# A graph network's preparation on one core: noise embedding and row splits on VectorE, weight pieces behind the tables, edges loaded first, waits on stored counts divided

## What is computed

```python
# cut to what matters; shapes: x [1250, 512], src, dst, edge_weight [21250], node_vec1 [1250, 1]
freqs = jnp.arange(1, 33) * (2.0 * np.pi / 16)
ph = noise_levels * freqs
emb = jnp.concatenate([jnp.sin(ph), jnp.cos(ph)], axis=-1)         # [1250, 64]
cond = silu(emb @ f_w1 + f_b1) @ f_w2 + f_b2                       # [1250, 16]
for i in range(4):
    y = layernorm(x) * (1 + cond @ s1_w[i] + s1_b[i]) + cond @ b1_w[i] + b1_b[i]
    y = sparse_attention(y, src, dst, ...)                         # softmax over each node's edges, 4 heads
    x = x + y
    y = layernorm(x) * (1 + cond @ s2_w[i] + s2_b[i]) + cond @ b2_w[i] + b2_b[i]
    x = x + relu(y @ m_w1[i] + m_b1[i]) @ m_w2[i] + m_b2[i]
x = layernorm(x0 + x)
agg = segment_sum(x[dst] * edge_weight[:, None], src)
return layernorm(x + agg @ weight.T)
```

## Time and profile before

| | |
|---|---|
| median of 3 runs | 1954.78 us (1954.19 to 1955.04) |
| profiled execution | 1956.64 us, its span 1954.8 us |
| granted TensorE clock, mean | 0.97 |
| busy: TensorE, VectorE, ScalarE, GpSimd | 1783.7, 1306.0, 916.6, 423.4 us |
| last group added, tables done | 247.7 us from the start of the span |
| first scores of layer 0 | 313.4 us |

### The profile page before, as it was taken

The page is one execution under the profiler, slowest core; times in us unless marked ns, Lnnn a source line. Parts: engine busy times, 40 slices in busy tenths (PEclk is TensorE's granted clock), DMA queues, the critical chain, the costliest instruction groups (busy, mean ns, idle before and its releaser), DMA issues.

```text
span 1954.8 us, 31300 instructions
## 1 busy us (share of the span) xinstructions
PE 1783.7 (91%) x11879; PEld 1527.7 (78%) x11879; DVE 1306.0 (67%) x2411; ACT 916.6 (47%) x1471; POOL 423.4 (22%) x499
## 2 busy tenths in 40 slices
PE   3447579999999999999999999999999999999898
PEld 3446557888888788888887888888878888888777
DVE  8997785676685655766856567668565676585744
ACT  6557664454454244544542445445424454453221
POOL 5562223000025230000251300002513000024300
PEclk9678789999999999999999999999999999999999
DMA  3020155242231022422410224223102233232122
GB/s 117 11 49 10 57 223 186 85 148 90 85 127 50 16 83 81 142 90 85 133 44 16 88 84 135 96 83 129 44 16 90 76 131 104 88 115 86 40 69 76
DMA packets 63635, 170.06 MB, mean 87 GB/s; under 512 B 5857, under 2 KB 24066, under 8 KB 63485
## 3 DMA queue, kind: packets, MB, share of 16 engines
q10 hardware_dynamic: 23040, 102.41, 15.6%
q1 hardware_dynamic: 40452, 65.69, 10.3%
HBM read 146.58 MB, written 17.02 MB: 84 GB/s over the span
## 4 chain that ended last, share of the span: by engine, by line
PE 75%; DVE 10%; issue 7%; ACT 3%; DMA 2%; DVEq 2%; SPq 1%; POOL 1%; POOLq 0%; ACTq 0%
PE ps L1442 65%; PE ps L1654 8%; DVE onehot L1032 1%; PE ps L1574 1%; DVE prob L1198 1%; DVE PT_lo L1214 1%; DVEq L1056 1%; DVE CW L1068 1%; ACT PT_hi L842 1%; DVE CW L1071 1%; DVE CW L1064 1%; DMA piece<-in_L_gnn_m_w_dram 1%; PE ps L1869 1%; DVE CW L1066 0%; SPq L388 0%
## 5 line engine op out<-in xcount | busy, mean ns | idle before, releaser
L842 ACT ACTIVATE PT_hi<-ps 128x512 fp32r<-128x512 f32 x400 | 238.5, 596 | 245.0 <-PE ps L1654 244.1
L1214 DVE TENSOR_TENSOR PT_lo<-ps,PT_hi 128x512 fp32r<-128x512 f32 x400 | 274.1, 686 | 50.0 <-ACT PT_hi L842 42.4
L826 ACT ACTIVATE prob<-prob,nmax 128x1250 f32<-128x1250 f32 x160 | 214.0, 1338 | 139.0 <-DVE nmax L1198 139.0
L1654 PE MATMUL ps<-ident,prob 128*128 128x128 f32 x1600 | 248.4, 278 | 11.9 <-DVE PT_lo L1214 11.9
L1198 DVE CUSTOM_DVE_ANT_0 prob<-ps,Lr 128x1250 f32<-128x1250 f32 x160 | 232.2, 1451 | 33.6 <-PE ps L1442 32.2
L1654 PEld LDWEIGHTS ps<-ident,prob 128*128 128x128 f32 x1600 | 181.7, 140 | 78.8 <-DVE PT_lo L1214 61.1
L1442 PE MATMUL ps<-PT_hi,v_hi 128*128 128x256 f32 x800 | 228.0, 285 | 1.1 <-DVE PT_lo L1214 1.1
L1442 PE MATMUL ps<-PT_lo,v_hi 128*128 128x256 f32 x800 | 226.1, 283 | 0.0
L1442 PE MATMUL ps<-PT_hi,v_lo 128*128 128x256 f32 x800 | 225.9, 282 | 0.0
L1442 PE MATMUL ps<-yT,wqk_hi 128*128 128x512 f32 (+1 forms) x768 | 213.0, 364 | 4.3 <-DVE yT L1151 4.3
L1442 PE MATMUL ps<-win,onehot 128*128 128x112 bf16 x1680 | 113.8, 240 | 101.0 <-DVE CW L1071 78.3
(11 more groups left out here) (205 smaller groups left out, 3797.5 us busy)
## 6 DMA issues: line engine op xcount, KB each, us to landing
Lr<-l_table ACTq DMA_DIRECT2D x160, 625.0 KB, 3.9
piece<-in_L_gnn_m_w_dram SPq DMA_DIRECT2D x32, 256.0 KB, 2.7
w_table<-CW SPq DMA_DIRECT2D x5, 1250.0 KB, 7.5
l_table<-CW SPq DMA_DIRECT2D x10, 625.0 KB, 3.2
prob<-w_table SPq DMA_DIRECT2D x10, 625.0 KB, 3.9
x<-in_x_dram SPq DMA_DIRECT2D x2, 2304.0 KB
CW<-CW SPq DMA_DIRECT2D x7, 625.0 KB, 5.8
piece<-in_L_gnn_wv_dram SPq DMA_DIRECT2D x16, 256.0 KB, 2.7
```

The lines of the kernel that those rows point to most:

```text
L826: act.activation(buf, buf, ACT.Exp, bias=nmax[:, i % 4:i % 4 + 1], scale=-1.0, accum_out=rsum[:, i % 4:i % 4 + 1]).then_inc(S["exped"], 1)
L842: act.activation(o, i, ACT.Copy).then_inc(S["pt_hi"], 1)
L1214: dve.tensor_tensor(lo, i, hi.bitcast(F32), ALU.subtract).then_inc(S["pt_split"], 1)
L1654: m = pe.transpose(bank(5 + n % 2, at * P, (at + 1) * P), prob[:, (NT * h + 2 * g + j) % 3, d * P:(d + 1) * P], ident[:])
```

## The change

1. **Angles on VectorE.** The embedding's angles are made by VectorE ahead of group 8 (`angles`), with fewer steps, since one instruction multiplies and adds. The nodes are folded into two halves: 128 x 640 in place of 64 x 1280. The sine, the noise matmuls (four in place of three) and the silus move from groups 28 to 32 to groups 12 to 17, the condition from 34 to 18.
2. **Row differences on VectorE**, ahead of groups 16 and 24; ScalarE's casts at groups 6, 22 and 28 in place of 3, 9 and 17.
3. **Weight pieces.** The six pieces are loaded into buffers of their own, without waiting for one another. ScalarE rounds them at groups 44 to 54; GpSimd subtracts all six after `tables_done`.
4. **Edges first.** SyncE loads the edges before it adds START to the semaphores. ScalarE casts `iota_h`; the constant rows of the stacks are copied by SyncE's queue; GpSimd zeroes three tiles, ScalarE nine.
5. **TensorE** turns the biases ahead of group 3 in place of ahead of group 0.
6. **VectorE's loop** is written out in seven parts; five row statistics instead of three are taken ahead of the last eight groups, and the two between the first normed rows are gone.
7. **Divided waits.** Four semaphores count the stores of logarithms in place of two, and `qk_hi_` waits for those that its own columns need. ScalarE's third logarithm and its store come earlier.

```diff
-ZERO_BY_DMA, ZERO_BY_POOL, ZERO_SOURCE = range(7), (7, 8), NT - 1
+ZERO_BY_POOL = ((1, 7), (1, 8), (0, 9))
+ZERO_BY_ACT = range(9)
-L_FIRST = 5
-ACT_L_AT = {1: (2,), 2: (3,), 3: (4,), ...}
+L_STORE = (0, 0, 1, 1, 2, 3, 3, 3, 3, 3)
+L_STORES = (2, 2, 1, 5)
+QK_STORES = {0: (0,), 1: (1,), 4: (2,)}
+ACT_L_AT = {2: (3,), 3: (4,), ...}
-EARLY_STATS = 3
+EARLY_STATS = 5
@@ SyncE
-            for s in counted:
-                sp.sem_inc(s, START)
             sp.wait_ge(pre_set, 2)
...
+            for s in counted_groups:
+                sp.sem_inc(s, START)
             sp.wait_ge(zero_source, 1)
...
+            for s in S.values():
+                sp.sem_inc(s, START)
...
-            for n in range(4):
-                load_piece(0, n)
+            for n in range(AHEAD_PIECES):
+                sp.dma_start(first_raw(n), piece_rows(0, n)).then_inc(first_in[n], 16)
...
-                if n == L_FIRST - 1:
-                    store_weights(4)
+                if n in (1, 2):
+                    store_weights(n + 2)
@@ GpSimd
-            between = {1: (constants, phase), 2: (lambda: row_rest(0), turns), ...}
+            between = {6: (cond_rest,), 9: (last_x,)}
...
+                    if l == 0 and t == EARLY_STATS - 1:
+                        pool.wait_ge(tables_done, 1)
+                        for n in range(AHEAD_PIECES):
+                            first_rest(n)
@@ ScalarE
-            between = {2: (biases,), 3: (lambda: row_hi(0),), 9: (lambda: row_hi(1),), 17: (lambda: row_hi(2),),
-                       24: (lambda: first_hi(0), lambda: first_hi(1)), 28: (sines,), 29: (lambda: silu(0), lambda: silu(1)),
-                       32: (lambda: silu(2),), 35: (cond_copy,), 41: ..., 43: (cond_stack,), 47: ...}
+            between = {4: (biases,), 6: (lambda: row_hi(0),), 12: (sines,), 14: (lambda: silu(0), lambda: silu(1)), 17: (lambda: silu(2), lambda: silu(3)),
+                       20: (cond_copy,), 22: (lambda: row_hi(1),), 28: (lambda: row_hi(2),), 31: (cond_stack,),
+                       **{44 + 2 * n: (lambda n=n: first_hi(n),) for n in range(AHEAD_PIECES)}}
...
                     if l == 0 and h == 0:
-                        act.wait_ge(l_stored1, 16 * L_FIRST)
+                        for i in QK_STORES.get(c, ()):
+                            act.wait_ge(l_stored[i], 16 * L_STORES[i])
...
+                    elif l == 0:
+                        log_counts(2)
@@ VectorE
-            dve.wait_ge(iota_set, 3)
-            link(dve.tensor_copy(iota_h[:], iota_i[:]))
...
+            def angles():
+                dve.wait_ge(noise_in, 32)
+                dve.wait_ge(f_set, 2)
+                dve.wait_ge(iota_set, 8)
+                link(dve.tensor_scalar(fcol[:, 0:1], fcol_i[:], TWO_PI / 16.0, None, ALU.mult))
+                link(dve.tensor_scalar(sin_a[:], sin_a[:], fcol[:, 0:1], None, ALU.mult))
...
+                for c in TURN:
+                    link(dve.scalar_tensor_tensor(out=sin_a[:], in0=sin_b[:], scalar=-c, in1=sin_a[:], op0=ALU.mult, op1=ALU.add))
+                link(dve.tensor_scalar(sin_a[:], sin_a[:], fcol[:, 2:3], PI_IN, ALU.add, ALU.min))
+                dve.tensor_scalar(sin_a[:], sin_a[:], -PI_IN, None, ALU.max).then_inc(sin_ready, 1)
...
+            between = {1: (angles,), 2: (lambda: row_rest(0),), 3: (lambda: row_rest(1),), NG // UNROLL_G - 1: (early_stats,)}
+
+            for i in range(NG // UNROLL_G - 1):
+                for work in between.get(i, ()):
+                    work()
+                with dve.If(flag < 1):
+                    groups(i)
...
-                        if t + 3 < NT:
+                        if EARLY_STATS <= t + 3 < NT:
                             stats(t + 3)
...
-                    first_stats(EARLY_STATS + step - 1)
                     log_table(step - 1)
+            log_table(2)
@@ TensorE
-            between = {29: (lambda: hidden_cond(0), lambda: hidden_cond(1)), 31: (lambda: hidden_cond(2),), 34: (make_cond,), 42: (turn_cond,)}
+            between = {3: (turn_biases,), 12: (lambda: hidden_cond(0), lambda: hidden_cond(1)), 15: (lambda: hidden_cond(2), lambda: hidden_cond(3)), 18: (make_cond,),
+                       29: (turn_cond,)}
```

More of the change, by code:

```diff
@@ L241, in build @@
             wv_hi = sb("wv_hi", [P, KT, D], F32R, start_of_layer)
+            with ExitStack() as prep:
+                wv_raw = sb("wv_raw", [P, KT, D], F32, prep)
             wv_lo = sb("wv_lo", [P, KT, D], F32R, start_of_layer)
@@ L276, in build @@
         piece_in = [sem(f"piece_in{i}") for i in range(2)]
+        first_in = [sem(f"first_in{i}") for i in range(AHEAD_PIECES)]
         stacks1_in, stacks2_in, bo_in = sem("stacks1_in"), sem("stacks2_in"), sem("bo_in")
@@ L297, in build @@
         x0_in = sem("x0_in")
-        l_stored1, l_stored2 = sem("l_stored1"), sem("l_stored2")
+        l_stored = [sem(f"l_stored{i}") for i in range(len(L_STORES))]
         l_in = [sem(f"l_in{i}") for i in range(LBUFS)]
@@ L353, in pieces, with first_raw @@
             return []
+        def first_raw(n):
+            return wv_raw[:, n, :] if n < QKO else wqk_raw[:, n - QKO]
         def piece_parts(n):
@@ L449, in _ @@
             sp.dma_start(x[0:LAST, NT - 1, :], T["x"][(NT - 1) * P:N, :]).then_inc(x_in, 16)
-            for n in range(4, AHEAD_PIECES):
-                load_piece(0, n)
             def store_weights(i):
@@ L598, in last_x @@
                 pool.memset(x[:, NT - 1, :], 0.0).then_inc(f_set, 1)
-            between = {1: (constants, phase), 2: (lambda: row_rest(0), turns), 3: (lambda: less(TURN[0]),),
-                       4: (lambda: row_rest(1),), 5: (lambda: less(TURN[1]),), 6: (lambda: less(TURN[2]), bounded),
-                       7: (lambda: first_rest(0), lambda: first_rest(1)), 10: (cond_rest,),
-                       11: (lambda: first_rest(2), lambda: first_rest(3)), 12: (last_x, lambda: first_rest(4), lambda: first_rest(5))}
+            between = {6: (cond_rest,), 9: (last_x,)}
             pool.wait_ge(eplan, 2)
@@ L710, in _ @@
             act.wait_ge(iota_set, 1)
-            for t in range(NT):
+            for t in ZERO_BY_ACT:
                 act.activation(CW[:, 0, t, :], nil[:].to_broadcast([P, N]), ACT.Copy).then_inc(zero_act, 1)
+                if t == 0:
+                    act.wait_ge(iota_set, 3)
+                    act.activation(iota_h[:], iota_i[:], ACT.Copy).then_inc(iota_cast, 1)
+            act.wait_ge(iota_cast, 1)
             def distance(group, q):
@@ L974, in _ @@
             dve.memset(CW[:, 1, ZERO_SOURCE, :], 0.0).then_inc(zero_source, 1)
-            dve.memset(fcol[0:32, 1:3], 0.0)
-            dve.memset(fcol[32:64, 1:2], 0.25)
-            dve.memset(fcol[32:64, 2:3], TWO_PI / 4).then_inc(f_set, 1)
+            for i in (0, 64):
+                dve.memset(fcol[i:i + 32, 1:3], 0.0)
+                dve.memset(fcol[i + 32:i + 64, 1:2], 0.25)
+                m = dve.memset(fcol[i + 32:i + 64, 2:3], TWO_PI / 4)
+            m.then_inc(f_set, 1)
             dve.memset(eT[:], -1.0).then_inc(dchain, 1)
```

184 lines of the change are left out of this document (88 added, 96 removed).

## The result

| | before | changed |
|---|---|---|
| median | 1954.91 us (1954.19 to 1958.67) | 1894.22 us (1893.53 to 1896.85) |
| profiled execution, span | 1954.8 us | 1891.7 us |
| ratio | | 0.9688, 95% interval 0.9672 to 0.9703 |

The spans of the two profiled executions differ by 63.1: the changed kernel's was the fastest of its four runs, while the profiled one of before took 1956.64 us, over its median. The busy times by stage of the changed kernel, with the columns of the earlier trace rows (the second stretch ends where VectorE first reads scores, 2.2 us after TensorE's first scores, where the earlier trace rows cuts): stretch and length, then TensorE's matmuls and weight loads, VectorE, ScalarE and GpSimd with the number of instructions, the granted clock, DMA share, GB/s.

What follows compares the result with a forecast made beforehand. The change is decided in the first 313 us, where VectorE sets the loop's pace, its compares stretched by GpSimd. Tables done 52.8 us earlier and 4 behind them give -56.8: 1898 us median, range 1887 to 1917.

Steps and rivals of the forecast that it cites:

- first addition: VectorE's first addition into CW in the loop over edge groups: at 19.1 us in place of 24.76, -5.7.
- the clean loop: The 56 edge groups without added work and remaining waits: 149.5 us, between 142.5 and 157.
- added on VectorE: Work VectorE takes on in the loop: angles 7.5, row differences 4.4, statistics 4.0, together 15.9 us.
- waits that stay: Loop waits around make_cond, noise matmuls, angles and VectorE's branches: 10.4 us, bounds 6 and 22.
- behind the tables: From the tables' end onward, with divided store waits and fewer statistics there: -4 us, bounds -8 and +1.
- the start: Before the loop: edge loads issued earlier move all that follows 2.1 us forward; with TensorE's earlier groups, -5.7 in all.
- The stretch: In the loop, GpSimd instructions lengthen VectorE's 119 one-hot compares by 51 us; the moved work's share goes.
- The 9.08 of before: Loop wait of 9.08 us behind ScalarE's one-hot, queued behind a late weight piece: claimed to go.
- (a): Rival: TensorE bounds the loop, at the lower clock for half the groups: 22 us, giving 1920; chance 0.12.
- (b): Rival: the compares' lengthening is not GpSimd's doing, none of 51 us returns: 1949; chance 0.04.
- (c): Rival: divided waits do nothing and weight pieces behind the tables hold the values: +5 to +8, 1905; chance 0.13.
- (d): Rival: slower than before, late inputs of moved work stop VectorE's loop; 65 us late gives 1963; chance 0.02.

Runs made afterwards that it cites:

- e10: Changed kernel with SyncE's semaphore increments (START) put back ahead of the edge loads: 1895.12 us against 1894.22.
- e11: Changed kernel with GpSimd's fills at the start held until the cast of the second edge list is done: 1893.19 us against 1894.22.
- e9: Changed kernel with the transpose of the bias rows ahead of group 0 on TensorE again: 1899.76 us against 1894.22.
- e1: Changed kernel with useless GpSimd work added in the loop, 24 scalings and 32 fillings of a 128x320 scratch tile: 1902.53 us against 1894.22.
- e3: Changed kernel with the two row differences on GpSimd again, at chunks 2 and 4 of the loop: 1906.92 us against 1894.22.
- e5: Changed kernel with useless GpSimd work added in the loop, 4 long scalings (128x1280 together) and 32 fillings: 1905.68 us against 1894.22.
- e12: Changed kernel with the six weight-piece subtractions back in the loop, in GpSimd's chunks 12 and 13: 1897.33 us against 1894.22.
- e2: Changed kernel with the angles on GpSimd again, still folded, and sines, noise matmuls and condition at later groups: 1898.35 us against 1894.22.
- e4: Changed kernel with one wait for all stored counts ahead of the first q, instead of three: 1898.87 us against 1894.22.

## Why the prediction was right, point by point

| step | forecast | profile of the changed kernel |
|---|---|---|
| first addition | 19.1 | 22.15 |
| the clean loop | 149.5 | 147.3 (167.65 less the next two rows) |
| added on VectorE | 15.9 | 15.3: angles 6.6, rows 4.5, statistics 4.2 |
| waits that stay | 10.4 | 5.0: of the 7.1 of L1060, 2.1 stand before the first group |
| tables done | 194.9 | 189.80 |
| TensorE's first scores | 257 | 249.68 |
| behind the tables | -4 | -5.2 (1707.1 to 1701.9): -5.8 up to the first scores, 0.6 more after them |

The direction and the loop's mechanism came as forecast. That the total came so near is in part luck: the start gave 3.1 us less than forecast, and the clean loop, the added work, the waits and the part behind the tables gave 2.2, 0.6, 5.4 and 1.2 more. For the profiled execution the forecast was 1899.8 and 1893.5 was measured.

- **The start failed as a step.** "The destination edges are what the plan waits for ... so all that follows moves 2.1 us forward" was read from a wait of 1.03 us in the earlier trace rows. What stood next behind it was not asked: three fills of tables on GpSimd, one more than before, and that of cstack, over the two casts. The forecast had the third fill, but weighed it only against the window products at 14.6. e10 and e11 show both halves. The step about the biases was right (4.15 in e9): TensorE now starts with GpSimd's first products, at 18.36. But these follow the window compare, which stayed where it was.
- **The stretch went, as forecast.** 51 us of stretching were read from 119 compares; 45.3 went, and 6 stayed beside the window products. The reading of the earlier trace rows was right: a compare ends with GpSimd's instruction. But the number does not follow from GpSimd's 67.5 us less work, as I first took it for e1. It comes from instructions of 3 to 4 us being gone: 40 us of the stretch before stood in fifteen rows over 1 us. e3 and e5 put sizes on that (7.2 us for two, 10.2 for four), e12 on those of 1.3 to 1.9 us, e1 and e2 the bound.
- **Waits were over-sized.** make_cond's 5.6 came out as 2.70, because a row difference covered 2.3 of it by luck of place (5.02 in e3, 5.05 in e2). The noise matmuls cost no wait. The 9.08 of before went as forecast: no row of ScalarE's stands behind a late weight piece any more. No run put the old loads of the pieces back, so that this was their doing is read from the two traces alone. Behind the angles TensorE stood idle for 7.69 us and then took 2.96 for a group, and VectorE did not wait for it. Branches cost about the 2.2 that was put down, in rows named "issue"; but the loop before had as much under that name.
- **The angles** took 0.49 us for a step with constants and 0.55 with a column as scalar, where 0.67 came from the earlier trace rows; the three combined steps took 0.83, not 0.76.
- **Behind the tables** the sum was near: the divided waits gave 4.7 by e4's median, of which the clock may hold a part, and two stretched table steps cost 0.8 and 0.4, together 1.2 where 0.7 was taken off. The rule of SBUF — State Buffer in the Trainium skill (section Who interferes with whom), that the holder keeps the ports for a whole instruction, agrees with the rows at 83.59 of e5 and 194.00; the whole turns of 2.8 us that it could have meant here did not occur.
- **The rivals.** (a) did not come: 0.94 was granted. (b) is refuted by e5, where added GpSimd work stretched the compares again. (c) is refuted by e4: with the waits undivided q_hi waits for a store again and the time rises. (d) did not come: no row of VectorE in the loop waits on a load.

## What to carry to other kernels

Price an engine's contention by the length of its single instructions, not by its busy time. Here 56 of 0.4 and 1.2 us, about as short as the gaps between the other engine's contending steps, cost 2.2 us in all; those of 1.3 to 1.9 cost 0.6 each; those of 3.5 to 4.4 cost most of their length wherever the other engine was not waiting anyway. Fold or cut a tile before moving it to the busy engine. And when a load is issued earlier, look at what holds the instruction behind it: the first load and the fills that held the cast had to move together for 2.15 us to appear.
